# The exact split of the row maxima moved from VectorE to GpSimd in a one-core attention kernel

## The chip, the cores and the metric

One core of one Trainium2 chip runs the whole program. The metric is the device time of one execution in microseconds (us), as the median of several executions; lower is better.

## The reference, cut to what matters

The program takes 4 batches of 512 tokens of width 512 through a weighted mixing layer, a quantised feed-forward layer, and then the layer with which this case deals, a cross-attention with 16 heads of width 32, followed by a last quantised linear layer:

```
q = qdq(x) @ qdq(wq).T + bq                 # qdq: rounded to 8 bits by row
k, v = split(cond @ wkv.T + bkv)
attn = softmax(einsum('bnhd,bmhd->bhnm', q, k) / sqrt(32))
o = einsum('bhnm,bmhd->bnhd', attn, v)
out = qdq(o) @ qdq(wp).T + bp
```

The softmax is kept safe by subtracting the row maximum of q.k before the exponential. Those maxima are needed to float32 precision though they travel as float16, so each is sent as two float16 numbers, a high part and the rest.

## The kernel before, in words

The attention part goes through 16 head groups, 4 batches times 4 groups of 4 heads; here they are numbered n = 0 to 15. Each group is walked in 16 slots, one for each pair of a block of 128 keys (t = 0 to 3) and a head (j = 0 to 3): slot = 4t + j. There is no planner; each engine has its own instruction order written out by hand, and semaphores tie them.

- TensorE, in `attend` (from L1302 on): in each slot it computes some score rows of the next group (`rows`, L1230, into three rotating banks), then the slot's transposed scores (`scores`, L1249, with 98 contraction rows: 96 for q and k, and 2 that add the negated maxima), into two alternating banks. In slots 5, 9 and 13 it multiplies weights and values (`weigh`, L1259), in slot 5 also the sums of the previous group (`sum_weights`, L1271), in slot 9 `c_turn` (L1238: it transposes the next group's 16 columns of negated maxima from 128 partitions to 4 rows of 512), in slot 10 `o_turn` (L1289), in slot 13 `sum_turn` (L1299). In even groups slot 3 has `sum_last` (L1281).
- ScalarE: one exponential per slot (L994), and behind the exponential of slot 9 `c_out` (L965), which copies the transposed maxima of the next group to float16: the high part.
- VectorE: the row maxima (`maxima`, L1728, 16 per group, of the next group; the last of the next group's are due in slot 7). In slot 7 `ints_ahead` (L1764, output integers of an earlier row block, groups 6 to 15), in slot 11 `c_low` (L1736: transposed maxima minus the high part, from PSUM), in slot 12 `bias_row` (L1795: adds a bias to one block of X in SBUF), in slot 13 an output row's maximum (L1782) with three short scale instructions, in slots 14 and 15 the inversion of sums and the normalisation (L1742, L1748).
- GpSimd: `add_weights` (L708) adds the exponentials up over the key blocks. Even groups have 12 additions of 128x512, odd groups 8; add (1,2) below is the third of a group, which follows the exponential of slot 6. Before the loop it has sent its memsets under the keys (L684).
- SyncE's queue: loads of keys and queries for later groups (L438 to L447), the transpose of the integers (`turn_o`, L514), and `send_c` (L463 to L465), which writes both parts of the maxima under the queries. The first score of the next group waits for that transfer.

Of the kernel before, what the change touches and what calls it, by code (L numbers as in the profile page):

```python
# [5 lines left out]
F32 = mybir.dt.float32  # L6
F16 = mybir.dt.float16
BF16 = mybir.dt.bfloat16
ALU = mybir.AluOpType
# [3 lines left out]
P = 128  # L13
BATCH, SEQ, D = 4, 512, 512
TOK = BATCH * SEQ // P
TB = SEQ // P
DB = D // P
# [6 lines left out]
HG = P // DH  # L24
# [7 lines left out]
def adds_before(b, g):  # L32

    return b * 40 + g * 12 - g // 2 * 4


def up_to(eng, sem, value):

    if isinstance(value, int) and value <= 0:
        return  # L40
    eng.wait_ge(sem, value)


class Chain:
# [11 lines left out]
    def turn(self, per_turn, k):  # L56

        self.before, self.per_turn = self.base + self.n, per_turn
        self.base, self.n = self.before + per_turn * k, 0
# [6 lines left out]
def flamingo_kernel(nc, x, ctx_2048, g_xattn, g_ffn, w, u, w1, w2, w3, wq, bq, wkv, bkv, wp, bp, gamma, wl, out):  # L66
    stack = ExitStack()
    with stack:
        def sb(name, shape, dt):
            return stack.enter_context(nc.sbuf_tensor(name, shape, dt))  # L70

        def sem(name):
            return stack.enter_context(nc.semaphore(name))
# [16 lines left out]
        id32 = sb("id32", [P, P], F32)  # L90
# [39 lines left out]
        def part(count, dt, pat=None, **kw):  # L130
            n16 = count * (2 if dt == F32 else 1)
            a = B[:, used[0]:used[0] + n16]
            used[0] += n16
            assert used[0] <= NB, used[0]
            if dt == F32:
                a = a.bitcast(F32)
            return a.rearrange(pat, **kw) if pat else a
# [37 lines left out]
        QS = A[:, 8192:16384].rearrange("p (h s) -> p h s", h=HEADS)  # L175
# [6 lines left out]
        QM, QSC, QR = part(4, F32), part(4, F32), part(4, F32)  # L182
        wm_raw = VB = part(TB * D, F32, "p (t d) -> p t d", t=TB)
        NMX = [part(16, F32, "p (t j) -> p t j", t=TB) for _ in range(2)]
        CT = [part(512, F16) for _ in range(2)]
        wm_ints = B[:, used[0]:used[0] + DB * D].rearrange("p (k d) -> p k d", k=DB)
        OT, SM = part(512, F32), part(512, F32)
        RDEN = part(16, F32)
# [22 lines left out]
        bank = [stack.enter_context(nc.psum_tensor(f"bank{n}", [P, 512], F32)) for n in range(8)]  # L211
# [42 lines left out]

        kv_in, q_in = [sem(f"kv_in{g}") for g in range(DB)], [sem(f"q_in{g}") for g in range(DB)]
        q_out = sem("q_out")
        ks_ones, row_ps, row_max, ct_low, c_ps, ct_ready, c_in = (
            sem("ks_ones"), sem("row_ps"), sem("row_max"), sem("ct_low"), sem("c_ps"), sem("ct_ready"), sem("c_in"))
        acc_done, sum_ps, x_biased = sem("acc_done"), sem("sum_ps"), sem("x_biased")
        st_ps, exp_done, pv_tile, ot_ready, sm_ready = sem("st_ps"), sem("exp_done"), sem("pv_tile"), sem("ot_ready"), sem("sm_ready")  # L260
        o_ps, s_ps, den_ready, o_norm = sem("o_ps"), sem("s_ps"), sem("den_ready"), sem("o_norm")
# [24 lines left out]
        AHEAD = 10  # L286
# [12 lines left out]
        def batches(eng, turn_):  # L299

            turn_(0, True, False)
            with eng.Fori(1, BATCH - 1) as b:
                turn_(b, False, False)
            turn_(BATCH - 1, False, True)
# [5 lines left out]
        def following(b, g):  # L310
            return (b, g + 1) if g < DB - 1 else (b + 1, 0)
# [42 lines left out]
        def _(sp):  # L354
# [105 lines left out]
            def send_c(b, g):  # L460

                sp.wait_ge(ct_ready, b * DB + g + 1)
                sp.wait_ge(ct_low, b * DB + g + 1)  # L463
                for h in range(2):
                    sp.dma_start(QS[96 + h:97 + h, HG * g:HG * g + HG, :], CT[h][0:HG, :]).then_inc(c_in, 16)  # L465

            def load_matrix(m):

# [71 lines left out]
        def _(pool):  # L540
            step = Chain(pool, pool_step)
# [152 lines left out]
            for u in (TOK - 3, TOK - 2, TOK - 1):  # L694
                q_low(u)
                ones_under(u - TOK + 4)

            def add_weights(b, first, last):
                for g in range(DB):
                    n, acc = b * DB + g, ACC[g % 2]  # L700
                    for t in range(1, TB - 1 if g % 2 else TB):
                        for j in range(HG):
                            pool.wait_ge(exp_done, n * 16 + HG * t + j + 1)
                            if t == 1:
                                up_to(pool, sum_ps, n - 1)
                            else:
                                pool.wait_ge(acc_done, adds_before(b, g) + HG * (t - 2) + j + 1)
                            nc.gpsimd.tensor_tensor(acc[j], PR[j] if t == 1 else acc[j], PR[(HG * t + j) % 8],  # L708
                                                    ALU.add).then_inc(acc_done, 1)

            batches(pool, add_weights)
            pool.wait_ge(x_biased, TOK)
            pool.wait_ge(swp_io, 32)

# [17 lines left out]
        def _(act):  # L732
            step = Chain(act, act_step)
# [227 lines left out]
            def c_out(b, g):  # L961
                n = b * DB + g
                act.wait_ge(c_ps, n + 1)
                up_to(act, c_in, n * 32)
                nc.scalar.copy(CT[0][0:HG, :], bank[4][0:HG, :]).then_inc(ct_ready, 1)  # L965

            def ot_out(b, g):
                n = b * DB + g
# [85 lines left out]
        def _(pe):  # L1054
            mm, turn = nc.tensor.matmul, nc.tensor.transpose
# [62 lines left out]
            for s in range(DB * BATCH):  # L1118
                b, k = divmod(s, DB)
# [5 lines left out]
                for p, j in parts:  # L1125
                    if p == 2 and j == 0:
                        pe.wait_ge(ctx_lo, DB * b + DB)
                    wt, cx = operands[p]
                    last_ = mm(bank[6][:, :], wt[:, j, k * P:k * P + P], cx[:, j, :],
                               start=(p == 0 and j == 0), stop=(p == 2 and j == DB - 1))  # L1130
# [4 lines left out]
                for p, j in parts:  # L1135
                    wt, cx = operands[p]
                    last_ = mm(bank[7][:, :], cx[:, j, k * P:k * P + P], wt[:, j, D:2 * D],  # L1137
                               start=(p == 0 and j == 0), stop=(p == 2 and j == DB - 1))
# [93 lines left out]

            def c_turn(b, g):
                n = b * DB + g
                pe.wait_ge(row_max, n * 16 + 16)
                up_to(pe, den_ready, n - 2)
                for t in range(TB):
                    last_ = turn(bank[4][0:HG, t * P:t * P + P], NMX[g % 2][:, t, :], id32[:, :])  # L1238
                last_.then_inc(c_ps, 1)

            def scores(b, g, t, j):
# [50 lines left out]
            def sum_turn(b, g):  # L1292

                n = b * DB + g
                pe.wait_ge(sm_ready, n + 1)
                pe.wait_ge(ct_ready, min(n + 3, DB * BATCH))
                pe.wait_ge(ct_low, min(n + 3, DB * BATCH))
                for t in range(TB):
                    last_ = turn(bank[4][:, t * P:t * P + P], SM[:, t * P:t * P + P], id32[:, :])  # L1299
                last_.then_inc(s_ps, 1)  # L1300
# [111 lines left out]
        def _(dve):  # L1412
            step = Chain(dve, dve_step)
            link = step.link
            ts, tt, stt = nc.vector.tensor_scalar, nc.vector.tensor_tensor, nc.vector.scalar_tensor_tensor
# [31 lines left out]
            for n in range(3):  # L1447
                last = nc.vector.tensor_copy(WG[:, n, :], WREST[:, :])
# [279 lines left out]
                reduce(NMX[g % 2][:, t, j:j + 1], bank[ROW_BANKS[r % 3]][:, :], AX.X, ALU.max,  # L1728
                       negate=True).then_inc(row_max, 1)

            def c_low(b, g):

                n = b * DB + g
                dve.wait_ge(ct_ready, n + 1)
                up_to(dve, c_in, n * 32)
                tt(CT[1][0:HG, :], bank[4][0:HG, :], CT[0][0:HG, :], ALU.subtract).then_inc(ct_low, 1)  # L1736

            def invert_sums(b, g):
                n = b * DB + g
                dve.wait_ge(s_ps, n + 1)  # L1740
# [25 lines left out]
            def attend(b, first, last):  # L1766
                for g in range(DB):
                    opening, closing = first and g == 0, last and g == DB - 1
                    ahead = coming(b, g)
                    for slot in range(16):  # L1770
                        for at, n in ahead[slot]:
                            maxima(at // DB, at % DB, n)
                        if slot == 11 and not closing:
                            c_low(*following(b, g))
                        if slot == 12:
                            bias_row(b * DB + g)
                        if slot == 7 and 0 <= b * DB + g - TB - 2 < AHEAD:
                            ints_ahead(b * DB + g - TB - 2)
                        if slot == 13 and 0 <= b * DB + g - TB - 1 < AHEAD:
                            i = b * DB + g - TB - 1  # L1780
                            dve.wait_ge(o_norm, i // TB * DB + DB)
                            link(reduce(OM[:, i:i + 1], OALL[:, i:i + 1, :], AX.X, ALU.max, apply_absolute_value=True))  # L1782
                            scales(i, i + 1)
                        if slot == 14 and not opening:
                            invert_sums(*preceding(b, g))
                        if slot == 15 and not opening:
                            normalize(*preceding(b, g))
                    if b * DB + g - TB >= AHEAD:
                        i = (b - 1) * TB + g
                        reduce(OM[:, bass.ds(i, 1)], OALL[:, bass.ds(i, 1), :], AX.X, ALU.max, apply_absolute_value=True)  # L1790

            def bias_row(i):

                row_ = flat(X[:, bass.ds(i, 1), :])
                tt(row_, row_, bp_all[:, :], ALU.add).then_inc(x_biased, 1)  # L1795
# [16 lines left out]
            q_full(TOK - 1)  # L1812
            first_maxima(8, 16)
            maxima(0, 1, 0)
            c_low(0, 0)
            for n in range(1, LEAD):
                maxima(0, 1, n)
            for b in range(BATCH):
# [6 lines left out]
            for t in range(TOK - TB, TOK):  # L1825
                last_ = reduce(OM[:, t:t + 1], OALL[:, t:t + 1, :], AX.X, ALU.max, apply_absolute_value=True)
# [91 lines left out]
```

## Time and profile before

| what | value |
|---|---|
| median of 3 runs | 925.54 us (925.45 to 925.75) |
| profiled execution, its own time | 926.48 us |
| its span, first to last instruction | 924.7 us |
| mean granted TensorE clock | 0.955 |
| busy: PE, DVE, ACT, POOL | 87%, 84%, 62%, 57% |
| attention part, first score of group 0 to last group | 572.9 to about 830 us |

PE is TensorE, DVE VectorE, ACT ScalarE, POOL GpSimd. A busy share is an average over parts of the program that have different limits. The profiled execution is one execution, 0.1% above the median; durations and distances below come from it.

### The profile page before, as it was taken

The numbers are of one execution on the slowest core, as the hardware profiler recorded it, in microseconds if no ns is written. First come the engines' busy times: TensorE is split into PE (matmuls) and PEld (weight loads), VectorE is DVE, ScalarE is ACT, GpSimd is POOL, SyncE is SP. The second block draws the span as 40 slices with busy tenths as digits, with TensorE's granted clock in tenths as the row PEclk, the third lists the DMA queues.
The fourth block names the chain that finished last, engine by engine and source line by source line (L and its number), as shares of the span: only waits on it lengthen the run. The fifth ranks groups of instructions, "written<-read, shape, count | busy, mean of one in ns | idle before, by whom it ended". The sixth has DMA issues, their size and how long they took to land.

```text
span 924.7 us, 14062 instructions
## 1 busy us (share of the span) xinstructions
PE 806.8 (87%) x4269; PEld 347.1 (38%) x4269; DVE 774.1 (84%) x1497; ACT 570.5 (62%) x969; POOL 525.2 (57%) x608
## 2 busy tenths in 40 slices
PE   3899997789899999999999987999999999974664
PEld 3445443334344444444444442223223222222221
DVE  4999998788899899899888768787889899847884
ACT  4888897343566555566666554666666666664762
POOL 7776763133344344445443344977887797796570
PEclk9999999799999999999999996999999999997885
DMA  9998976423344363463433364422132321010111
GB/s 310 253 229 208 235 215 156 125 57 58 74 111 67 73 121 69 86 75 72 89 78 72 57 146 83 103 61 79 49 96 58 98 59 53 7 13 1 68 47 68
DMA packets 192426, 92.03 MB, mean 100 GB/s; under 512 B 144080, under 2 KB 176992, under 8 KB 192352
## 3 DMA queue, kind: packets, MB, share of 16 engines
q1 hardware_dynamic: 192032, 91.13, 41.5%
q8 instruction: 34, 0.56, 0.3%
q14 instruction: 40, 0.33, 0.2%
q10 hardware_dynamic: 320, 0.01, 0.0%
HBM read 44.05 MB, written 16.78 MB: 66 GB/s over the span
## 4 chain that ended last, share of the span: by engine, by line
DVE 38%; PE 31%; issue 14%; ACT 9%; POOL 4%; DMA 2%; SPq 1%; DVEq 0%; ACTq 0%; POOLq 0%
PE bank L1167 10%; DVE B L1728 5%; PE bank L1179 5%; POOL B L708 4%; DVE bank L1602 3%; PE bank L1259 3%; DVE gsm L1604 3%; PE bank L1371 3%; DVE B L1613 3%; PE bank L1230 3%; PE bank L1249 2%; DVE B L1607 2%; ACT bank L862 2%; ACT A L994 2%; DVE gsm L1605 1%
## 5 line engine op out<-in xcount | busy, mean ns | idle before, releaser
L1167 PE MATMUL bank<-A,B 128*128 128x512 f16 x1024 | 232.6, 380 | 13.1 <-DVE B L1613 12.7
L639 POOL TENSOR_TENSOR B<-B 128x512 f16<-128x512 f32 x64 | 75.7, 1183 | 215.3 <-DVE B L1613 133.9
L994 ACT ACTIVATE A<-bank 128x512 f32<-128x512 f32 x256 | 143.2, 601 | 83.7 <-PE bank L1249 80.9
L1728 DVE TENSOR_REDUCE B<-bank 128x1 f32<-128x512 f32 x256 | 162.0, 681 | 35.7 <-PE bank L1230 35.6
L1167 PEld LDWEIGHTS bank<-A,B 128*128 128x128 f16 x1024 | 99.2, 98 | 138.6 <-DVE B L1613 15.6
L708 POOL TENSOR_TENSOR B<-B,A 128x512 f32<-128x512 f32 x96 | 125.8, 1342 | 0.0
L1179 PE MATMUL bank<-A,B 128*128 128x512 f16 x512 | 120.6, 379 | 0.0
L862 ACT ACTIVATE bank<-B 128x512 f32<-128x512 f32 x64 | 38.5, 602 | 130.6 <-DVE B L1607 130.6
L708 POOL TENSOR_TENSOR B<-A 128x512 f32<-128x512 f32 x64 | 81.5, 1296 | 54.6 <-ACT A L994 54.6
L1230 PE MATMUL bank<-A 96*128 96x512 f16 x256 | 100.7, 404 | 6.4 <-DVE B L1728 3.9
L1249 PE MATMUL bank<-A 98*128 98x512 f16 x256 | 96.3, 388 | 11.1 <-ACT A L994 8.5
L1259 PE MATMUL bank<-A,B 128*32 128x512 f32 x512 | 68.6, 608 | 2.0 <-ACT A L994 1.0
L1179 PEld LDWEIGHTS bank<-A,B 128*128 128x128 f16 x512 | 49.5, 98 | 54.3 <-DMA B<-B 0.3
L1137 PE MATMUL bank<-B 128*128 128x512 f16 x192 | 48.2, 405 | 14.8 <-DVE B L1493 14.5
L1602 DVE SCALAR_TENSOR_TENSOR bank<-bank,ffs,B 128x512 f32<-128x512 f32 x64 | 48.4, 756 | 12.2 <-PE bank L1167 11.0
L1613 DVE SCALAR_TENSOR_TENSOR B<-bank,gsm 128x512 f32<-128x512 f32 x64 | 44.3, 691 | 16.0 <-ACT bank L862 14.0
L588 POOL TENSOR_SCALAR B<-X,mv,rs 128x128 f32<-128x128 f32 x64 | 54.2, 858 | 0.2
L857 ACT ACTIVATE B<-bank,ffs 128x512 f32<-128x512 f32 x64 | 43.3, 676 | 17.4 <-PE bank L1167 17.1
L1230 PEld LDWEIGHTS bank<-A 96*128 96x128 f16 x256 | 25.0, 100 | 71.5 <-DVE B L1728 46.2
L1249 PEld LDWEIGHTS bank<-A 98*128 98x128 f16 x256 | 24.9, 98 | 60.7 <-ACT A L994 39.1
L1604 DVE TENSOR_REDUCE gsm<-bank 128x8 f32<-128x512 f32 x64 | 44.3, 692 | 2.2
L1607 DVE TENSOR_TENSOR B<-bank,gsm 128x512 f32<-128x512 f32 x64 | 44.2, 691 | 2.2
(217 smaller groups left out, 1457.2 us busy)
## 6 DMA issues: line engine op xcount, KB each, us to landing
B<-in_L_ffn_w_dram SPq DMA_DIRECT2D x48, 256.0 KB, 3.5
A<-k_parts SPq DMA_DIRECT2D x48, 128.0 KB, 2.7
A<-q_parts SPq DMA_DIRECT2D x48, 128.0 KB, 3.7
X<-in_x_dram SPq DMA_DIRECT2D x4, 1024.0 KB, 8.9
B<-in_ctx_dram SPq DMA_DIRECT2D x16, 256.0 KB, 5.0
k_parts<-B SPq DMA_DIRECT2D x16, 256.0 KB, 4.4
v_rows<-B SPq DMA_DIRECT2D x16, 256.0 KB, 2.8
q_parts<-B SPq DMA_DIRECT2D x32, 128.0 KB, 2.2
```

The costliest lines, as they stand in the source:

```text
L639: nc.gpsimd.tensor_tensor(HLb[j][:, 1, :], Db[j % 2], HLb[j][:, 0, :], ALU.subtract).then_inc(lo_done, 1)
L708: nc.gpsimd.tensor_tensor(acc[j], PR[j] if t == 1 else acc[j], PR[(HG * t + j) % 8], ALU.add).then_inc(acc_done, 1)
L994: nc.scalar.activation(PR[(HG * t + j) % 8], bank[2 + j % 2][:, :], ACT.Exp, scale=SCALE).then_inc(exp_done, 1)
L1167: last = mm(bank[2 * n + q][:, :], XQT[a][:, m, :], wt[:, m % DB, j * 512:j * 512 + 512], start=(m == 0), stop=(m == 2 * DB - 1))
L1179: last = mm(bank[5 + q][:, :], HT[j][:, m, :], W3T[:, DB * j + m % DB, :], start=(j == 0 and m == 0), stop=(j == FC - 1 and m == 2 * DB - 1))
L1230: mm(bank[ROW_BANKS[r % 3]][:, :], QS[0:96, HG * g + j, t * P:t * P + P], KS[0:96, HG * g + j, :], start=True, stop=True).then_inc(row_ps, 1)
L1249: mm(bank[2 + j % 2][:, :], KS[0:98, HG * g + j, t * P:t * P + P], QS[0:98, HG * g + j, :], start=True, stop=True).then_inc(st_ps, 1)
L1259: last_ = mm(bank[6][DH * j:DH * j + DH, :], VB[:, t, (HG * g + j) * DH:(HG * g + j + 1) * DH], PR[(HG * t + j) % 8], start=(t == 0), stop ...
L1602: stt(H, H, C2, SAb[q], ALU.mult, ALU.mult).then_inc(h_done, 1)
L1604: link(reduce(gsm[:, 0, :], grouped(H), AX.X, ALU.max, apply_absolute_value=True))
L1613: stt(grouped(Db[q]), grouped(bank[q][:, :]), RND, spread(1), ALU.subtract, ALU.mult).then_inc(d_done, 1)
L1728: reduce(NMX[g % 2][:, t, j:j + 1], bank[ROW_BANKS[r % 3]][:, :], AX.X, ALU.max, negate=True).then_inc(row_max, 1)
```

## The change

VectorE's `c_low` goes. In its place GpSimd has a new step, `c_split`, of three short instructions on 16 columns, behind its add (1,2): round the negated maxima to float16, widen that again into columns 0 to 3 of a 32-column tile, and put the difference into columns 4 to 7. TensorE then turns 8 columns rather than 4, and waits for GpSimd's step (`c_parts`) rather than for VectorE's last maximum (`row_max`); ScalarE's one copy turns all 8 rows to float16, and SyncE sends both parts once that copy is done. Two other steps of VectorE change place: `bias_row` from slot 12 to slot 5, and `ints_ahead` from slot 7 to slot 9. GpSimd's hardware loop over the two middle batches is written out.

```
-        CT = [part(512, F16) for _ in range(2)]
+        CT = part(512, F16)
+        NHL = [part(32, F32, "p (t c) -> p t c", t=TB) for _ in range(2)]
+        NHI = part(16, F16, "p (t j) -> p t j", t=TB)
...
                 sp.wait_ge(ct_ready, b * DB + g + 1)
-                sp.wait_ge(ct_low, b * DB + g + 1)
...
-                    sp.dma_start(QS[96 + h:97 + h, HG * g:HG * g + HG, :], CT[h][0:HG, :]).then_inc(c_in, 16)
+                    sp.dma_start(QS[96 + h:97 + h, HG * g:HG * g + HG, :], CT[HG * h:HG * h + HG, :]).then_inc(c_in, 16)
...
+            def c_split(b, g):
+                n = b * DB + g
+                pool.wait_ge(row_max, n * 16 + 16)
+                up_to(pool, c_ps, n - 1)
+                step.link(nc.gpsimd.tensor_scalar(NHI, NMX[g % 2], 1.0, 0.0, ALU.mult, ALU.add))
+                nc.gpsimd.tensor_scalar(NHL[g % 2][:, :, 0:HG], NHI, 1.0, 0.0, ALU.mult, ALU.add)
+                nc.gpsimd.tensor_tensor(NHL[g % 2][:, :, HG:2 * HG], NMX[g % 2], NHI, ALU.subtract).then_inc(c_parts, 1)
...
+                            if (t, j) == (1, 2) and not (last and g == DB - 1):
+                                c_split(*following(b, g))
...
-            batches(pool, add_weights)
+            c_split(0, 0)
+            for b in range(BATCH):
+                add_weights(b, b == 0, b == BATCH - 1)
...
-                nc.scalar.copy(CT[0][0:HG, :], bank[4][0:HG, :]).then_inc(ct_ready, 1)
+                nc.scalar.copy(CT[0:2 * HG, :], bank[4][0:2 * HG, :]).then_inc(ct_ready, 1)
...
-                pe.wait_ge(row_max, n * 16 + 16)
+                pe.wait_ge(c_parts, n + 1)
...
-                    last_ = turn(bank[4][0:HG, t * P:t * P + P], NMX[g % 2][:, t, :], id32[:, :])
+                    last_ = turn(bank[4][0:2 * HG, t * P:t * P + P], NHL[g % 2][:, t, :], id32[:, :])
...
-            def c_low(b, g):
-
-                n = b * DB + g
-                dve.wait_ge(ct_ready, n + 1)
-                up_to(dve, c_in, n * 32)
-                tt(CT[1][0:HG, :], bank[4][0:HG, :], CT[0][0:HG, :], ALU.subtract).then_inc(ct_low, 1)
...
-                        if slot == 11 and not closing:
-                            c_low(*following(b, g))
-                        if slot == 12:
+                        if slot == 5:
                             bias_row(b * DB + g)
-                        if slot == 7 and 0 <= b * DB + g - TB - 2 < AHEAD:
+                        if slot == 9 and 0 <= b * DB + g - TB - 2 < AHEAD:
                             ints_ahead(b * DB + g - TB - 2)
```

## Rows read from the trace of the kernel before

**Rows 1.** The page: its head, and part 4, the chain that ended last, by engine.
```profile
span 924.7 us, 14062 instructions
...
DVE 38%; PE 31%; issue 14%; ACT 9%; POOL 4%; DMA 2%; SPq 1%; DVEq 0%; ACTq 0%; POOLq 0%
```
**Rows 2.** Timeline of ACT: start and duration in us, and idle time before, with what ended it.
```profile
630.58 0.57 ACT L965 CAST B<-bank 4x512 f16<-4x512 f32 x1 [0.54 <-PE bank L1238]
...
646.71 0.57 ACT L965 CAST B<-bank 4x512 f16<-4x512 f32 x1 [0.54 <-PE bank L1238]
...
662.26 0.57 ACT L965 CAST B<-bank 4x512 f16<-4x512 f32 x1 [0.54 <-PE bank L1238]
...
809.11 0.57 ACT L965 CAST B<-bank 4x512 f16<-4x512 f32 x1 [0.54 <-PE bank L1238]
```
**Rows 3.** The chain of waits, 640 to 662 us (group 4, into group 5): start, us, what.
```profile
646.15 0.55 PE bank L1238 x4
646.71 0.45 ACT B L965
...
657.67 0.86 PE bank L1271 x8
```
**Rows 4.** The chain of waits, 699 to 717 us (group 8).
```profile
709.13 1.30 DVE B L1764
...
712.23 0.59 DVE B L1736
...
713.41 1.15 DVE X L1795
```
**Rows 5.** Timeline of POOL, groups 4 and 8.
```profile
649.21 1.71 POOL L708 TENSOR_TENSOR B<-B,A 128x512 f32<-128x512 f32 x1
...
655.79 1.27 POOL L708 TENSOR_TENSOR B<-B,A 128x512 f32<-128x512 f32 x1
...
706.15 1.28 POOL L708 TENSOR_TENSOR B<-A 128x512 f32<-128x512 f32 x1 [5.83 <-ACT A L994]
...
708.88 1.27 POOL L708 TENSOR_TENSOR B<-A 128x512 f32<-128x512 f32 x1 [0.23 <-ACT A L994]
```
**Rows 6.** Timeline of DVE, group 4.
```profile
643.34 2.49 DVE L1728 TENSOR_REDUCE B<-bank 128x1 f32<-128x512 f32 x4 [1.54 <-PE bank L1230]
...
648.73 1.07 DVE L1795 TENSOR_TENSOR X<-X,bp_all 128x512 f32<-128x512 f32 x1
```
**Rows 7.** Timeline of POOL, short instructions in earlier parts of the program.
```profile
65.16 0.19 POOL L561 TENSOR_SCALAR rs<-mv 128x4 f32<-128x4 f32 x1
...
66.72 3.13 POOL L588 TENSOR_SCALAR B<-X,mv,rs 128x128 f32<-128x128 f32 x4
...
542.19 0.40 POOL L651 TENSOR_TENSOR B<-id,B 128x128 f32<-128x128 f32 x1
...
543.94 0.19 POOL L645 TENSOR_TENSOR nm<-mv,rs 128x1 f32<-128x1 f32 x1
544.21 0.19 POOL L646 TENSOR_TENSOR sh<-held,nm 128x1 f32<-128x1 f32 x1
```
**Rows 8.** Timeline of all engines, start of the attention part.
```profile
567.11 1.80 POOL L684 MEMSET A<- 2x2048 f16 x1
...
567.52 1.01 PE L1238 MATMUL bank<-id,B 128*4 128x128 f32 x4 [1.42 <-DVE B L1728]
...
570.35 1.41 SPq L465 DMA_DIRECT2D A<-B  x2
...
572.90 0.61 PE L1249 MATMUL bank<-A 98*128 98x512 f16 x1 [0.17 <-DMA A<-B]
```
**Rows 9.** Timeline of PE, group 8, the turn of the maxima.
```profile
710.66 0.60 PE L1238 MATMUL bank<-id,B 128*4 128x128 f32 x4
```
**Rows 10.** The chain of waits, 757 to 830 us, end of group 14's additions.
```profile
818.59 1.72 POOL B L708
...
820.35 1.06 PE bank L1271 x8
```

More of the change, by code:

```diff
@@ L256, in flamingo_kernel @@
         q_out = sem("q_out")
-        ks_ones, row_ps, row_max, ct_low, c_ps, ct_ready, c_in = (
-            sem("ks_ones"), sem("row_ps"), sem("row_max"), sem("ct_low"), sem("c_ps"), sem("ct_ready"), sem("c_in"))
+        ks_ones, row_ps, row_max, c_parts, c_ps, ct_ready, c_in = (
+            sem("ks_ones"), sem("row_ps"), sem("row_max"), sem("c_parts"), sem("c_ps"), sem("ct_ready"), sem("c_in"))
         acc_done, sum_ps, x_biased = sem("acc_done"), sem("sum_ps"), sem("x_biased")
@@ L1296, in sum_turn @@
                 pe.wait_ge(ct_ready, min(n + 3, DB * BATCH))
-                pe.wait_ge(ct_low, min(n + 3, DB * BATCH))
                 for t in range(TB):
@@ L1814, in _ @@
             maxima(0, 1, 0)
-            c_low(0, 0)
             for n in range(1, LEAD):
```

## The prediction

> **What bounds the kernel now.** I read first the page. Its chain of waits [rows 1] shares the span between VectorE (38%) and TensorE (31%), with GpSimd at 4%: over the whole program no engine can take on work for nothing. The change touches only the attention part, so next I measured its period there, in the timeline of ScalarE. The copy of the turned maxima (L965) occurs once a group in slot 9 and makes a good clock [rows 2]. From group 3 to group 4 it advances 16.13 us, from 4 to 5 15.55 us: even groups have one more product. From 662.26 (group 5) to 809.11 (group 14) it advances 146.85 us over nine groups, five into even ones and four into odd ones. At the early pace these would take 5 x 16.13 + 4 x 15.55 = 142.85 us. So the later groups lose 4.0 us in all, 0.44 each.
>
> Then I read the chain of waits itself, in an early and in a late group. In group 4 [rows 3] it goes over TensorE and ScalarE: the turn of the maxima (L1238), straight into ScalarE's copy. ScalarE has been idle for 0.54 us before each such copy, waiting for the turn [rows 2], and its next exponentials stand behind that copy in its order. There is no slack: a turn that starts later moves the copy, the exponentials of slots 10 and 11, the score that waits for them and the next product. In group 8 [rows 4] the chain lies on VectorE, without a break from slot 7 over the integers (1.30 us), `c_low` (0.59) and the bias (1.15) into the next group. That is what the late groups' 4.0 us are: VectorE has the integers, an output maximum and scales there on top, and reaches the score rows of the next group late.
>
> **What the change takes away.** VectorE loses `c_low`, 0.59 us a group [rows 4]. The bias leaves slot 12, where it stood on the late groups' chain for 1.15 us [rows 4], and goes to slot 5. Behind slot 5's maximum VectorE is idle for 1.54 us, until the row behind TensorE's two products [rows 6]; the bias takes 1.07 there now, so it is covered, unless it must wait for GpSimd (below). The integers move from in front of slot 8's maximum to behind slot 9's, still ahead of `c_low`'s old place. In all the late groups' VectorE gets rid of 1.74 us behind slot 7, four times the 0.44 that these groups lose. I take the loss as wholly given back: **-4.0 us**. It can't give more by this reading, since the early groups run at their pace with VectorE idle before its maxima [rows 6], held by TensorE and ScalarE. For the early groups the relief is costed at nothing for that reason.
>
> **What it adds: a step on GpSimd ahead of the turn.** The turn used to wait for the last maximum of slot 7, which ended before the integers began at 709.13 [rows 4], 1.5 us ahead of the turn at 710.66 [rows 9]: no wait at all. Now it waits for GpSimd. Add (1,2) of group 8 ends at 708.88 + 1.27 = 710.15 [rows 5], 0.51 us before the turn, and the same distance holds for groups 1 to 14. So a step of length S ends in time only if S plus the hand-over is at most 0.51.
>
> S is three instructions on 16 columns and one wait of GpSimd for itself. The trace has none on 16 columns. From below: 0.19 us each, the price of 1 and of 4 columns [rows 7], and 0.08 for the wait (0.19 from 543.94, next at 544.21): 0.65, or 0.57 if they overlap by the 0.04 that GpSimd's neighbours show. From above: on a line between 4 and 128 columns (0.19 to 0.79 for one input, four in 3.13; 0.40 for two inputs) [rows 7], 0.25 + 0.25 + 0.22 + 0.08 = 0.80. I take 0.70, between. The hand-over from GpSimd to TensorE is 0.04 without a weight load in front (820.31 to 820.35) [rows 10]; I take 0.08.
>
> **And a collision.** The bias reads and writes SBUF, and so does every addition. In the trace the addition that starts under a bias takes 1.71 us rather than 1.27 [rows 5], and the bias ends 0.59 us after that addition's start whatever its own start (648.73 + 1.07 = 649.80, 649.21 + 0.59) [rows 5, 6]. So a bias waits until the addition in flight is over, and then the next one waits 0.44 us. All 16 biases show it. In slot 12 this fell on late additions. In slot 5 it falls on add (1,0) or (1,1): GpSimd starts at 706.15 [rows 5], within 0.2 us of where VectorE gets free. Only 0.23 us of idle time stand ahead of add (1,2) [rows 5], so 0.44 - 0.23 = 0.21 goes to the end of add (1,2). The Trainium skill, "SBUF — State Buffer", section "SBUF: two separate sides", has the rule behind it: a VectorE operation with two SBUF inputs and a GpSimd operation share one pair of ports as an exclusive lock, held for the whole instruction by whichever starts first. This case's rows agree (1.71 against 1.27 us). Without such a lock the forecast would be 4.8 us lower. The bias itself then ends 0.59 after add (1,1)'s start, about when slot 6's maximum is due: under 0.1 us, not on the chain.
>
> From group 6 on the integers in slot 9 meet the new step too. They hold a following addition for 0.18 us by the trace (1.45 instead of 1.27, all ten times); now it is the first instruction of the step. I call that 0.18 for groups 6 to 14.
>
> So the turn comes later by D = 0.21 + 0.70 + 0.08 - 0.51 = **0.48 us**, and by 0.66 in groups 6 to 14. Groups 0 to 14, fifteen turns: 15 x 0.48 + 9 x 0.18 = **+8.8 us**.
>
> **The other queues.** GpSimd's nine additions behind the step end later by 0.70 + 0.21 - 0.44 = 0.47 us, since the bias no longer falls on them. In group 4 they end at 657.06 [rows 5] and the sums that wait for them start at 657.67 [rows 3], itself later by 0.48: covered, and odd groups have four additions fewer. The parts' transfer needs no `c_low` now, 0.59 us less, while SyncE's transpose for the integers is issued about 1.2 us later and ahead of it: these about cancel. It landed some 1.1 us before the score that waits for it. Nothing. Eight columns in the turn instead of four: the moving side is unchanged, nothing.
>
> **The start.** The first turn began at 567.52 [rows 8]. `c_split(0, 0)` stands behind GpSimd's last memset, which ends at 568.91 [rows 8]: the turn begins at 568.91 + 0.70 + 0.08 = 569.69, 2.17 us later. The copy follows by 1.7 us, and its end at 571.4 releases the transfer, which was issued at 570.35 [rows 8] behind `c_low`. So it leaves 1.1 us later, and the first score, which waits for just this at 572.90 [rows 8], with it: **+1.1 us**. **The end.** The sums of slot 5 of group 15 start 0.04 us after GpSimd's last addition of group 14 [rows 10], one of 1.72 us under a bias. That wait shrinks as group 15 itself starts later: **-0.2 us**.
>
> **The sum.** 8.8 - 4.0 + 1.1 - 0.2 = +5.7 us. The profiled execution took 926.48 with a span of 924.7; it is 0.9 above the median, and I add the difference to the median: 925.54 + 5.7 = **931.2 us**, slower by 0.6%.
>
> **Rivals.**
> - *The split fits into the gap (0.16).* S at 0.57, hand-over 0.08, and no lock in slot 5 or 9: D = 0.14, then 2.1 - 4.0 + 1.0 - 0.2 = -1.1, 924.4 us. For it: no short GpSimd instruction in the trace is over 0.2 us without a power or 128 columns. Against: the lock shows under every bias.
> - *The split is dear (0.14).* S at 0.80 and the whole 0.44 on the path, if the idle 0.23 is gone: D = 0.81. 12.2 + 1.6 - 4.0 + 1.2 - 0.2 = +10.8, 936.3 us.
> - *VectorE's relief is worth more (0.10), the side of faster.* If the late groups' chain gave back all of the 1.74 us rather than 0.44, that is 9 x 1.74 = 15.7 instead of 4.0, and the time 931.2 - 11.7 = 919.5 us. It decides for faster by over 0.2% from 1.27 us a late group on. For it: the chain lies on VectorE without a break in group 8. Against: the early groups are without that load and no faster than 0.44.
> - The change does what it says in any case; that it is wholly neutral would need two of these to cancel.
>
> **Chances and range.** The forecast has 0.60, its own range 929 to 933.5. A change of under 0.2%, 1.85 us, can't be told from none here; so same is 923.7 to 927.4. Faster: the relief rival and a little of the first, 0.11. Same: most of the first, 0.13. Slower: 0.76. The range, 925.0 to 935.5, leaves out the relief rival, the lowest part of the first and the top of the second.
>
> **What would show it.** Right: L965 rows with 1.0 to 1.2 us of idle time before them instead of 0.54; the turn waiting for GpSimd in every group; three short POOL rows of 0.2 to 0.25 us; the 1.7 us additions at the group's second place instead of a late one; late groups at 15.55 and 16.13 plus 0.66; first score at 574.0. Wrong: L965's idle time still near 0.54, a period of late groups under 16.0 on average, VectorE idle in them for much more than 2 us a group with TensorE waiting for nothing.

## The result, and the profile after

The changed kernel takes 929.63 us as the median of 20 runs, the kernel before 925.61 us in 20 runs beside them: slower, with a ratio of 1.0037 (95% interval 1.0021 to 1.0053), 1.9 to 4.9 us. Single executions of either kernel spread over 8 to 11 us. The profiled one of the changed kernel took 927.53 us with a span of 925.6.

A good part of that spread lies ahead of anything that the change touches: VectorE's last maximum for group 0 ends at 567.38 us in the profile of before and at 563.72 in that of after, and anywhere from 562.6 to 569.2 in the profiles further down. Of the 3.7 us between the two, 3.0 are there when VectorE starts its 120th instruction, at 86.1 and 83.1 us. The five profiles of kernels with the split on VectorE have this maximum at 567.4 to 569.2, the seven with it on GpSimd at 562.6 to 567.6; whether that is chance or has to do with the change was not tested. So I compare from that maximum on. In the groups the periods repeat within some 0.02 us from one profile to the next, where the clock is the same.

The same four stretches of both, in the view that adds up busy time by window: from that maximum to the first score of group 0; from there to the first score of group 15; group 15 to its last exponential; the rest. Columns: window, its length, then busy time and instruction count of PE, weight loads, DVE, ACT and POOL, the granted clock, the DMA share and GB/s. The kernel before:

```profile
567.38:572.90 5.52, 4.63 (x12) 1.23 (x12) 3.90 (x7) 0.57 (x1) 1.53 (x1) 0.50 0.01 1
572.90:813.74 240.84, 227.61 (x1286) 68.88 (x1286) 203.45 (x343) 157.65 (x292) 190.19 (x148) 0.99 0.25 64
813.74:829.46 15.72, 11.30 (x64) 2.94 (x64) 5.10 (x6) 10.53 (x20) 15.72 (x13) 1.00 0.04 8
829.46:924.70 95.24, 53.53 (x248) 22.45 (x248) 67.67 (x169) 46.64 (x67) 47.23 (x33) 0.75 0.12 45
```

The changed kernel:

```profile
563.72:570.59 6.87, 4.42 (x11) 1.33 (x12) 2.94 (x6) 0.57 (x1) 2.14 (x4) 0.50 0.00 1
570.59:812.96 242.37, 225.22 (x1286) 68.90 (x1285) 195.81 (x329) 157.68 (x292) 197.27 (x193) 0.99 0.24 64
812.96:829.80 16.84, 12.70 (x64) 3.11 (x64) 3.27 (x6) 10.53 (x20) 16.18 (x13) 0.90 0.04 8
829.80:925.60 95.80, 55.24 (x248) 22.80 (x248) 67.24 (x169) 46.14 (x68) 46.90 (x32) 0.78 0.12 44
```

These add up to +4.6 us, in four parts: +1.35 at the start, +1.53 over fifteen groups, +1.12 in group 15, where the granted clock is 0.90 instead of 1.00, and +0.56 behind it. VectorE has 7.6 us less to do in the groups and GpSimd 7.1 more, and the groups are longer all the same.

The clock of the prediction, ScalarE's copy of the turned maxima (timeline of ACT), now reads as follows; it answers to [rows 2]:

```profile
646.19 0.57 ACT L978 CAST B<-bank 8x512 f16<-8x512 f32 x1 [0.82 <-PE bank L1251]
...
662.03 0.57 ACT L978 CAST B<-bank 8x512 f16<-8x512 f32 x1 [0.83 <-PE bank L1251]
...
678.54 0.57 ACT L978 CAST B<-bank 8x512 f16<-8x512 f32 x1 [0.92 <-PE bank L1251]
694.46 0.57 ACT L978 CAST B<-bank 8x512 f16<-8x512 f32 x1 [0.91 <-PE bank L1251]
```

ScalarE waits 0.82 us for the turn in early groups and 0.92 in late ones, instead of 0.54. That is the new wait, 0.28 and 0.38 us. Between 678.54 and 694.46 lie 15.92 us where the kernel before had 16.02: in late groups the relief of 0.47 just covers it. In early groups, with no relief, 15.84 stand against 15.55.

Why the turn is late is in the chain of waits of group 8, which lay on VectorE before [rows 4] and now goes over GpSimd into the turn (`issue` is time in which the engine waits for nothing that the profile shows):

```profile
708.27 1.27 POOL B L717
709.54 0.17 POOL B L703
...
710.06 0.22 POOL B L705
710.28 0.04 issue
710.33 0.61 PE bank L1251 x4
...
710.97 0.45 ACT B L978
```

Add (1,2) is over at 709.54, the split at 710.28, the turn starts 0.05 later. TensorE's row of the turn names its releaser; before it had none [rows 9]:

```profile
710.33 0.60 PE L1251 MATMUL bank<-id,B 128*8 128x128 f32 x4 [0.31 <-POOL B L705]
```

The collision, in the timelines of POOL and DVE of group 8:

```profile
706.60 1.71 POOL L717 TENSOR_TENSOR B<-A 128x512 f32<-128x512 f32 x1
...
709.80 0.30 POOL L704 TENSOR_SCALAR B<-B 128x16 f32<-128x16 f16 x1
```

```profile
705.59 1.60 DVE L1798 TENSOR_TENSOR X<-X,bp_all 128x512 f32<-128x512 f32 x1
707.22 2.48 DVE L1740 TENSOR_REDUCE B<-bank 128x1 f32<-128x512 f32 x4
709.62 0.42 DVE L1769 TENSOR_SCALAR B<-B 128x512 f16<-128x512 f32 x1
711.18 0.69 DVE L1740 TENSOR_REDUCE B<-bank 128x1 f32<-128x512 f32 x1 [1.15 <-PE bank L1243]
```

Add (1,1) takes 1.71 us under the bias, and one instruction of the split is stretched from 0.20 to 0.30 by the integers. These took 1.30 us in slot 7 [rows 4], in flight beside a long addition; beside the short instructions in slot 9 they take 0.42. VectorE then waits 1.15 us for TensorE: it is no longer the bound.

### The profile page after: what moved, and what is told of

It is laid out like the page before. It is cut to its first block, busy times and chain, and to the rows that moved or that the text cites. A ratio compares the mean times of both kernels' runs of the same rounds, so it can differ in the third digit from the quotient of the medians.

```text
span 925.6 us, 13992 instructions
## 1 busy us (share of the span) xinstructions
PE 805.7 (87%) x4269; PEld 346.7 (37%) x4269; DVE 763.5 (82%) x1481; ACT 569.7 (62%) x969; POOL 532.9 (58%) x656
## 4 chain that ended last, share of the span: by engine, by line
DVE 30%; PE 24%; issue 17%; POOL 13%; ACT 12%; DMA 1%; SPq 0%; ACTq 0%; DVEq 0%; POOLq 0%
POOL B L717 11%; PE bank L1180 11%; PE bank L1192 5%; ACT A L1007 4%; PE bank L1383 3%; DVE bank L1614 3%; DVE gsm L1616 3%; DVE B L1625 3%; DVE B L1619 2%; ACT bank L875 2%; DVE gsm L1617 1%; DVE bank L1560 1%; DVE B L1498 1%; PE bank L1251 1%; DVE bank L1552 1%
## 5 line engine op out<-in xcount | busy, mean ns | idle before, releaser
L717 POOL TENSOR_TENSOR B<-B,A 128x512 f32<-128x512 f32 x96 | 119.1, 1274 | 0.0
L717 POOL TENSOR_TENSOR B<-A 128x512 f32<-128x512 f32 x64 | 86.6, 1374 | 48.4 <-ACT A L1007 48.4
```

## The experiments

Lines such as `L965` and `L978` are the same statement in kernels whose lines are numbered differently. "Groups" is the time from the first score of group 0 to that of group 15, "start" and "group 15" as above, all from each kernel's profile. The ratio is to the kernel before, timed beside it.

| kernel | start | groups | group 15 | ratio (95% interval) |
|---|---|---|---|---|
| before | 5.52 | 240.84 | 15.72 | 1 |
| changed | 6.87 | 242.37 | 16.84 | 1.0037 (1.0021 to 1.0053) |
| both moves only | 5.53 | 237.53 | 15.40 | 0.9954 (0.9931 to 0.9978) |
| split only | 6.97 | 249.61 | 15.54 | 1.0133 (1.0107 to 1.0159) |
| split one addition earlier | 6.87 | 243.65 | 15.90 | 1.0069 (1.0043 to 1.0096) |
| split longer | 7.44 | 250.69 | 15.53 | 1.0135 (1.0110 to 1.0161) |
| changed, turn in slot 10 | 7.26 | 242.37 | 20.55 | 1.0044 (1.0026 to 1.0062) |
| moves only, turn in slot 10 | 5.53 | 239.71 | 17.71 | 0.9974 (0.9957 to 0.9992) |
| changed, first split ahead of memset | 5.33 | 242.09 | 15.53 | 0.9998 (0.9981 to 1.0015) |
| changed, once more | 7.26 | 242.76 | 16.83 | one run |
| bias moved only | 5.54 | 236.25 | 15.39 | 0.9968 (0.9952 to 0.9984) |
| integers moved only | 5.54 | 240.87 | 15.73 | 1.0008 (0.9987 to 1.0030) |

### The two moves without the split

```
-                        if slot == 12:
+                        if slot == 5:
                             bias_row(b * DB + g)
-                        if slot == 7 and 0 <= b * DB + g - TB - 2 < AHEAD:
+                        if slot == 9 and 0 <= b * DB + g - TB - 2 < AHEAD:
```

> The kernel before with nothing but the two moves: bias to slot 5, integers to slot 9; c_low stays on VectorE in slot 11. Theory A (the turn waits for GpSimd's split; the moves alone are pure relief): the turn stays where it was, 10.45 us behind an even group's first score and 9.85 behind an odd one's, all later groups run at the early pace of 16.13 and 15.55 us, so the attention part is shorter by about 4.0 us and the whole by 0.4%. Theory B (the collision of bias and integers with the additions is what costs): add (1,2) ends 0.1 us later and groups are longer than before by 0.1 to 0.3 us each, +2 to +4 us. Theory C (the cost lies outside the groups, in the start and in a clock that falls at the end): the groups as in A.

The periods from group 2 to group 13 are 16.13 and 15.55 us, early and late alike, and ScalarE's wait for the turn is back at 0.54:

```profile
648.28 0.57 ACT L965 CAST B<-bank 4x512 f16<-4x512 f32 x1 [0.54 <-PE bank L1238]
...
711.63 0.57 ACT L965 CAST B<-bank 4x512 f16<-4x512 f32 x1 [0.54 <-PE bank L1238]
```

Theory A holds: 3.3 us less in the groups, 0.46% less in all. Theory C expects the same of these groups; against it stand the 4.84 us by which the changed kernel's groups are longer than these. Add (1,2) does end later by 0.1 us, as B wants, but nothing waits for it here. One group is off the expectation, group 1, with 16.46 us instead of 15.84: its bias takes 2.8 us, of which more below. The 4.84 us are the price of the split on GpSimd: 0.28 us in each of groups 2 to 5, 0.38 in groups 6 to 13, 0.46 in group 14, 0.22 in group 0 and nothing in group 1, which takes 16.46 us in both.

### The split without the moves

The same two lines, undone in the changed kernel.

> The changed kernel with bias back in slot 12 and integers back in slot 7: only the split on GpSimd is left. Theory A: the step (0.66 us in the trace) follows add (1,2) with no lock ahead of it, so the turn is late by 0.66 + 0.06 - 0.51 = 0.21 us instead of 0.28 and 0.37; the late groups get rid of c_low alone (0.59 us), which is still more than the 0.47 that they lose, so they run at 16.34 and 15.75. Against the kernel before: 15 x 0.21 - 4.0 + 1.3 at the start = +0.5 us, not to be told from it; against the changed kernel about 3 us less. Theory B: the same turn wait matters little, and without the collision the groups lose nothing at all: about -4 us. A third possibility: the two moves carry the relief, then the late groups stay at 16.4 to 16.8 and the whole is 3 to 6 us over the kernel before.

The third possibility came true, and worse than expected: the groups take 8.8 us more than before the change, and the whole 1.3%. In early groups the turn is late by 0.18 us, close to the 0.21 of theory A. But late groups take 17.22 and 16.63 us, 0.6 more than before the change. My step from "VectorE loses 0.59 us" to "the late groups win" was wrong. VectorE in group 8 (timeline of DVE):

```profile
711.68 1.27 DVE L1740 TENSOR_REDUCE B<-bank 128x1 f32<-128x512 f32 x2
713.20 0.69 DVE L1740 TENSOR_REDUCE B<-bank 128x1 f32<-128x512 f32 x1 [0.24 <-PE bank L1243]
714.29 0.69 DVE L1740 TENSOR_REDUCE B<-bank 128x1 f32<-128x512 f32 x1 [0.40 <-PE bank L1243]
714.90 1.61 DVE L1798 TENSOR_TENSOR X<-X,bp_all 128x512 f32<-128x512 f32 x1
```

The bias of the same group in the kernel before:

```profile
713.34 1.22 DVE L1795 TENSOR_TENSOR X<-X,bp_all 128x512 f32<-128x512 f32 x1
```

VectorE's chain used to run through here without a break [rows 4]. Now TensorE, held at the turn, brings the rows late, so VectorE waits 0.64 us in the middle of its own chain, which eats `c_low`'s 0.59. And the additions stand elsewhere, so that the bias waits longer for the one in flight: 1.61 us instead of 1.22. From the first maximum behind its wait of 1.54 us in group 8 to the first one behind the next normalisation VectorE takes 10.50 us, against 9.87 before the change. The turn, too, is later in late groups than in early ones, since the integers in slot 7 stretch the split's first instruction from 0.20 to 0.38 us. A late turn and a chain on VectorE add up, where I had taken the longer of the two. Theory B is refuted by the sign: with the collision back in its old place the kernel is slower, not faster.

### The split one addition earlier

```
-                            if (t, j) == (1, 2) and not (last and g == DB - 1):
+                            if (t, j) == (1, 1) and not (last and g == DB - 1):
```

> The changed kernel with the split one addition earlier, behind add (1,1) instead of (1,2). There it waits for VectorE's last maximum (9.00 us behind an even group's first score) and ends at about 9.7, before TensorE comes to the turn at 10.45. Theory A: no wait in front of the turn, groups at 16.13 and 15.55, so about 5.1 us less than the changed kernel and 2.5 us less than the kernel before, 923 us. Theory B: additions (1,2) onwards start 0.9 us later, and GpSimd's queue sets the pace: no gain over the changed kernel, or a loss. Theory C: no gain.

In even groups it is as theory A said: the turn is at 10.45 us again, with no wait for GpSimd, and early periods are 16.14. But theory B is right on the rest. Additions behind the split start 0.95 us later, the next, odd group finds GpSimd still at work (its first addition starts at 5.85 us instead of 5.27), late even groups take 16.33, and the odd ones 15.8 to 16.0. Two of them, groups 5 and 9, take 17.22 and 17.43. The timelines of DVE and POOL in group 9 show why:

```profile
723.64 1.87 DVE L1740 TENSOR_REDUCE B<-bank 128x1 f32<-128x512 f32 x3
725.43 3.14 DVE L1798 TENSOR_TENSOR X<-X,bp_all 128x512 f32<-128x512 f32 x1
728.50 1.87 DVE L1740 TENSOR_REDUCE B<-bank 128x1 f32<-128x512 f32 x3
```

```profile
723.06 2.51 POOL L717 TENSOR_TENSOR B<-B,A 128x512 f32<-128x512 f32 x2
725.52 2.51 POOL L717 TENSOR_TENSOR B<-A 128x512 f32<-128x512 f32 x2
729.86 0.20 POOL L703 TENSOR_SCALAR B<-B 128x16 f16<-128x16 f32 x1 [1.83 <-DVE B L1740]
```

The bias, issued 0.09 us ahead of the start of the addition at 725.5, does not get between the additions at 725.5 and at 726.8; it is through only when both are, after 3.14 us. The last maxima come that much later and GpSimd in turn waits 1.83 us for them. So the split's place is squeezed from both sides: earlier it delays the additions and with them the sums (5.93 us behind an odd group's first score instead of 5.70) and, in two groups, the last maxima; later it delays the turn. That the late even groups take 16.33 us with the turn in time is not explained by these rows.

### The split made longer

```
                 step.link(nc.gpsimd.tensor_scalar(NHI, NMX[g % 2], 1.0, 0.0, ALU.mult, ALU.add))
+                for _ in range(2):
+                    step.link(nc.gpsimd.tensor_tensor(held[:, 0:1], held[:, 1:2], held[:, 1:2], ALU.add))
```

> The changed kernel with two more short GpSimd instructions, each waited for, inside the split (0.19 + 0.08 us each, 0.54 in all). They write a scratch column that nothing uses. Theory A: every one of 15 turns is later by the whole 0.54 and the time grows by 8.1 us over the changed kernel, plus 0.5 at the start. Theory B and C: the turn has slack or the cost is elsewhere, and the growth is under 3 us.

The timeline of POOL, the step in group 8:

```profile
714.61 0.20 POOL L703 TENSOR_SCALAR B<-B 128x16 f16<-128x16 f32 x1
714.89 0.56 POOL L705 TENSOR_TENSOR held<-held 128x1 f32<-128x1 f32 x2
715.53 0.20 POOL L706 TENSOR_SCALAR B<-B 128x16 f32<-128x16 f16 x1
715.70 0.22 POOL L707 TENSOR_TENSOR B<-B 128x16 f32<-128x16 f32 x1
```

and ScalarE's copy behind it:

```profile
716.61 0.57 ACT L980 CAST B<-bank 8x512 f16<-8x512 f32 x1 [1.47 <-PE bank L1253]
```

ScalarE waits 1.47 us, 0.56 more than in the changed kernel. The groups grow by 8.32 us over the changed kernel, 0.555 for each of 15, and the start by 0.57. Every nanosecond of the split is on the path, as theory A has it, and both rivals' bound of 3 us is passed. The whole grows from 1.0037 to 1.0135, some 9 us by the ratios, and by 7.4 us from profile to profile, where group 15 is shorter by 1.3 us at the full clock.

### The turn in slot 10

```
-                        if slot == 9 and not closing:
+                        if slot == 10 and not closing:
                             c_turn(*following(b, g))
...
-                            if (t, j) == (2, 1) and not closing:
+                            if (t, j) == (2, 2) and not closing:
                                 c_out(*following(b, g))
```

> The changed kernel with the turn of the maxima one slot later on TensorE (slot 10, behind o_turn) and its copy one exponential later on ScalarE (behind that of slot 10). The split ends 10.66 to 10.77 us behind an even group's first score; TensorE would now come to the turn at about 11.3. Theory A (the groups' loss is the wait of the turn for GpSimd): that wait is gone, ScalarE no longer idles for the turn either, and the groups run at the pace of the moves alone, 237.5 us from the first to the last group's first score instead of 242.4, or a little less; the start still costs 1.3, so about 0.25% faster than the kernel before. Rival: the parts now reach the queries too late and the next group's first score waits for the transfer, or GpSimd's own queue sets the pace: groups at 240 us or more.

> The kernel before with the two moves, and in addition the turn in slot 10, its copy behind the exponential of slot 10, and c_low in slot 12. There is no wait for GpSimd in it. If the 0.54 us for which ScalarE idles before the copy are themselves on the path, the groups get shorter by up to 0.5 each, 230 to 234 us instead of 237.5, and the whole is 1% faster than the kernel before. If not, it is as the moves alone, 0.5% faster.

In the second of these, with `c_low` still on VectorE (in slot 12) and nothing to wait for, the groups take 16.33 and 15.74 us instead of 16.13 and 15.55. So slot 10 is a worse place by 0.20 us a group in itself. ScalarE's wait for the turn does fall, from 0.54 to 0.22 us, and yet the groups get longer: my hope that this wait could be won was wrong. The first has the same 16.33 and 15.74 in nine of its groups (2 to 6, 8 to 10 and 12): the wait for GpSimd is gone altogether there. The timeline of PE in group 8 shows the turn directly behind `o_turn` without any idle time:

```profile
714.32 0.60 PE L1302 MATMUL bank<-id,B 128*128 128x128 f32 x4
714.76 0.60 PE L1251 MATMUL bank<-id,B 128*8 128x128 f32 x4
```

That bears out the mechanism, but not the 237.5 us that I had expected: it gives 242.37. Besides the 0.20 a group, three odd groups (7, 11 and 13) take 16.57 us, with biases of 2.7 us, long ones as in the experiment with the split one addition earlier. Against its own comparison, the moves with the turn in slot 10, the split still costs 2.66 us, and 2.5 of them lie in these three groups. And group 15 takes 20.55 us at a granted clock of 0.67. In the other kernel with the turn in slot 10 the clock fell in group 15 too, in the view by window:

```profile
813.11:830.82 17.71, 14.07 (x64) 3.29 (x64) 4.99 (x6) 10.51 (x20) 15.88 (x13) 0.81 0.04 7
```

### The first split ahead of the memset

`c_split(0, 0)` goes in front of GpSimd's last `ones_under`, with a wait for it behind.

```
-            for u in (TOK - 3, TOK - 2, TOK - 1):
+            for u in (TOK - 3, TOK - 2):
                 q_low(u)
                 ones_under(u - TOK + 4)
+            q_low(TOK - 1)
...
             c_split(0, 0)
+            pool.wait_ge(c_parts, 1)
+            ones_under(3)
```

> The changed kernel with the very first split ahead of GpSimd's last memset under the keys instead of behind it. Theory A: only the start changes. From VectorE's last first-group maximum to the first score it took 5.5 us before and 6.9 changed; with the split ahead of the memset the turn starts about 0.9 us behind that maximum instead of 2.45, so 5.3 to 5.6 us, and the time falls by 1.3 us, with the groups at 242.4 as in the changed kernel. Rival: something else sets the start (the clock, the rows' own pace), and it stays at 6.9.

The start takes 5.33 us, 1.54 less than in the changed kernel. The timeline of POOL, first of the changed kernel, then of this one:

```profile
563.47 1.80 POOL L685 MEMSET A<- 2x2048 f16 x1
565.35 0.21 POOL L703 TENSOR_SCALAR B<-B 128x16 f16<-128x16 f32 x1
```

```profile
565.98 0.21 POOL L704 TENSOR_SCALAR B<-B 128x16 f16<-128x16 f32 x1
...
566.72 1.80 POOL L685 MEMSET A<- 2x2048 f16 x1
```

The whole is 0.9998 of the kernel before, some 3.6 us under the changed kernel by the ratios, each of which is known to 1.5 us. That is more than the start, and the profile shows where some of the rest can be: group 15 takes 15.53 us at full clock, 1.3 less. The times inside groups 5 to 14, measured from each one's first score, agree with the changed kernel's within 0.02 us.

### The changed kernel once more

> The changed kernel once more, for a second profile. The groups should again take 242.4 us within 0.1, since they are set by instruction times alone. In the first profile group 15 took 16.84 us, 1.1 more than before, with TensorE's granted clock at half for 3.4 us in it. If that belongs to the change, it is there again; if it is a matter of when the clock is granted in one execution, group 15 takes 15.4 to 15.9 as in the other experiments.

Group 15 of this second profile, in the view by window, and under it the 3.4 us of the first profile in which the clock was halved:

```profile
812.62:829.45 16.83, 12.68 (x64) 3.08 (x64) 3.27 (x6) 10.53 (x20) 16.19 (x13) 0.90 0.04 8
```

```profile
821.50:824.90 3.40, 3.38 (x12) 0.70 (x13) 0.00 (x0) 1.93 (x4) 3.40 (x4) 0.50 0.00 0
```

Twice the same, within 0.01 us: it is no accident of one execution. Some 2 us before the clock falls to its lower level, 1.2 GHz, TensorE has waited for GpSimd's last additions. The timeline of PE at that place, in the changed kernel, the kernel before, and the one with the early first split:

```profile
819.38 1.06 PE L1284 MATMUL bank<-B,ones 128*32 128x512 f32 x8 [1.45 <-POOL B L717]
```

```profile
820.35 1.06 PE L1271 MATMUL bank<-B,ones 128*32 128x512 f32 x8 [1.63 <-POOL B L708]
```

```profile
819.74 1.07 PE L1287 MATMUL bank<-B,ones 128*32 128x512 f32 x8 [1.44 <-POOL B L718]
```

The latter two keep 2.4 GHz through group 15. So the length of this wait alone doesn't decide it. The third differs from the first in group 15 by nothing that I found but the time at which the group starts, which suggests that the place in time has a part. Of the twelve profiles four fell in group 15: the two of this kernel and those of the two kernels with the turn in slot 10, in one of which this wait is only 1.09 us. What decides was not tested and stays open.

The groups took 242.76, 0.39 more than in the first profile and not the 0.1 that I allowed. The whole of it lies in group 1, which took 16.84 us instead of 16.46 at the full granted clock, with a bias of 3.19 us instead of 0.73. Group 1 in the view by window, and then its bias in the timelines of DVE, of this profile and of the first:

```profile
585.39:602.23 16.84, 15.07 (x85) 4.51 (x86) 13.17 (x19) 10.29 (x20) 16.59 (x16) 1.00 0.48 121
```

```profile
591.15 3.19 DVE L1798 TENSOR_TENSOR X<-X,bp_all 128x512 f32<-128x512 f32 x1
```

```profile
591.88 0.73 DVE L1798 TENSOR_TENSOR X<-X,bp_all 128x512 f32<-128x512 f32 x1
```

Both biases start 5.76 us behind the group's first score, with an addition in flight and the next one 0.14 us away. One got in ahead of that addition and the other only behind it and the one that followed. So what a bias costs can differ between two executions of one kernel, and my premise that instruction times alone set the groups was not quite right.

### One move at a time

> The kernel before with the bias moved to slot 5 and nothing else. The moves together gave every late group back its 0.47 us. Theory A1 (the late groups' chain lies on VectorE behind slot 7, so only what leaves that stretch counts): the bias alone takes 1.15 us out of it, more than 0.47, and gives the whole relief: 16.13 and 15.55 us, groups at about 237.4 us, 0.45% faster than the kernel before. Rival A2 (the integers' collision with the additions in slot 7 counts too): late groups at 16.2 to 16.4 us.

> The kernel before with the integers moved to slot 9 and nothing else. Theory A1: they stay in the stretch behind slot 7 that is VectorE's chain and only change place with two maxima; the late groups keep 16.6 and 16.0 us within 0.1 and the whole is not to be told from the kernel before. Rival A2: the integers in slot 9 fall into the 1.10 us for which VectorE otherwise waits there, and the late groups win 0.2 to 0.4 us each, up to 4 us in all.

With the bias alone the groups run at 16.13 and 15.55 us, early and late, and take 236.25 us. With the integers alone they take 240.87, where the kernel before has 240.84, with 16.61 and 16.02 in late groups. The busy times by window, of the stretch of the groups, bias only and then integers only:

```profile
574.73:810.98 236.25, 223.79 (x1286) 68.87 (x1286) 210.30 (x343) 157.61 (x292) 190.04 (x148) 0.99 0.27 65
```

```profile
572.92:813.79 240.87, 227.62 (x1286) 68.87 (x1286) 203.43 (x343) 157.61 (x292) 190.22 (x148) 0.99 0.25 64
```

VectorE is busy for 210.3 us in the faster and 203.4 in the slower one, for the most part since a bias that waits for an addition counts as busy: the biases of groups 0 to 14 add up to 21.8 and 16.7 us. All of the relief is the bias's. (With the bias alone groups 0 and 1 are 1.3 us shorter than with both moves: group 0 has a granted clock of 0.86 instead of 0.78, and the bias of group 1 takes 0.96 us instead of 2.82.) The integers' move gives nothing, as theory A1 says; rival A2 is refuted on both.

No run here shows a form of the split on GpSimd that beats the kernel before. What beats both kernels is the bias in slot 5 without the split: 0.46% with both moves, 0.32% with the bias alone, two figures whose intervals overlap.

## Why the prediction was right, point by point

**The bound, and the relief.** Late groups were held by VectorE's chain behind slot 7 and lost 4.0 us. The moves alone bring every late group to the early pace, and the bias alone suffices. Right, in place and in size, for the late groups. Over all fifteen the two moves give 3.3 us, since group 1 loses 0.6 with its bias of 2.8 us, which I had not seen coming. The rival by which VectorE's relief is worth more is refuted: without the load behind slot 7 the groups come to 15.55 and 16.13 us and not below.

**The wait of the turn for GpSimd.** Right in mechanism: it appears in every group, and the longer split passes on to the time in full. I had put the delay D at 0.48 us, and at 0.66 in late groups; measured, it is 0.28 and 0.38. The terms: the split took 0.66 to 0.67 us where nothing collides, against my 0.70 (0.20, 0.20 and 0.22 for the three, nearly the price of one column). The hand-over took 0.05, against 0.08. The collision with the bias cost 0.10 on the end of add (1,2) against 0.21: add (1,1) grew by the whole 0.44 as I had said, but GpSimd's idle time in front of add (1,2) is 0.23 us only where add (1,0) starts 5.95 us behind an even group's first score; where it starts at 5.85, as it does in all of the changed kernel's even groups from 2 on, 0.33 us are free. The integers stretched the split by 0.10 instead of 0.18, since they met a short instruction and not a long one. So the two collision terms are the step that was mis-sized: 0.39 us in a late group, and 0.20 measured. By my terms the groups should have grown by 8.8 - 4.0 = 4.8 us; they grew by 4.84 - 3.31 = 1.53. The split's cost was forecast nearly twice as high as it is.

**The start.** +1.35 us against +1.1, and the memset's place is the cause: with the split in front of it the start is 5.33 us.

**The end.** Here a step failed. I had -0.2 us for group 15, and it took 1.12 more, at a granted clock of 0.90. At the full clock the term comes out: with the first split ahead of the memset group 15 takes 15.53 us, 0.19 less than before, and the sums do start earlier behind the group's first score. What I had left out is that the clock can fall there: 3.4 us at half clock outweigh it. Why it falls in this kernel stays open. A further 0.56 us behind group 15 I can't attribute: that stretch takes 93.5 to 96.5 us in the profiles of kernels that do the same there.

**The sum.** 5.7 us predicted; 4.6 in the profiles from the last maximum of group 0 on, 4.0 between the medians. The sum is closer than its terms, and that is luck: 3.3 us too much in the groups are partly made up by 1.3 too little in group 15, 0.6 behind it and 0.3 at the start. The first rival (the split fits into the gap) is refuted by the turn's releaser, and so is the dear one: the split is nearer to its lower bound.

**The other queues.** Costed at nothing, and nothing showed. The parts land 2.1 us ahead of the first score that needs them in groups 2 to 14, against 1.1 before.

## What to carry to other kernels

A step that goes to another engine costs by where its result is due, not by the engine's load: here 7 us of work on an engine that is idle for some 50 us of this stretch cost 4.8 us of time, because it ended some 0.3 to 0.4 us behind the moment at which TensorE comes to it, in nearly every group. Before a step is moved, measure the distance between the end of the work in front of it on the new engine and its consumer; what exceeds it was paid in full here. And test a change's parts by themselves: of three edits in this one, one gave all of the gain, one gave nothing, and one lost more than the gain.

## What the runs showed of the hardware

- A VectorE operation with two SBUF inputs does not simply wait for one GpSimd addition. Issued at the end of one, it was passed over at the next border too and took 3.14 us beside two further additions, the last 0.54 of them behind the second addition. In other groups it got in at the first border, at 1.60 us.
- GpSimd's short instructions hardly grow from 1 to 16 columns: 0.19 to 0.20 us with one input, 0.19 to 0.22 with two.
- The half clock in group 15 came in both profiles of one kernel, behind a wait of 1.45 us, and not in the one profile of a kernel whose instructions differ from it only at the start of the attention part and in the time at which that group begins (a wait of 1.44 us).
- Which addition a waiting VectorE operation gets behind can differ from one execution to the next: in group 1 of the changed kernel the bias, issued at the same 5.76 us with an addition due 0.14 us later, took 0.73 us in one and 3.19 in the other.
